# Attention block with GroupNorm: the inverse of the softmax sums computed on 128 x 4 elements instead of 128 x 512

## The chip, the cores and the metric

The kernel runs on one core of one Trainium2 chip. The metric is the device time of one execution in microseconds (us); lower is better. Beside the timed runs there is one execution taken by the hardware profiler, and all rows below are from it. Engines: PE is TensorE's matmul, PEld its weight load, DVE is VectorE, ACT is ScalarE, POOL is GpSimd and SP is SyncE, which only sends transfers here.

## The reference

Sixteen images of 512 channels by 32 x 32 positions (1024 tokens) pass through one attention block:

```python
h = group_norm(hidden_states, norm_gamma, norm_beta)      # 32 groups, eps 1e-6
q, k, v = conv1x1(h, wq, bq), conv1x1(h, wk, bk), conv1x1(h, wv, bv)
attn = jnp.einsum('bci,bcj->bij', qf, kf) * 512 ** -0.5
attn = jax.nn.softmax(attn, axis=2)
out = jnp.einsum('bcj,bij->bci', vf, attn)
return hidden_states + conv1x1(out, wo, bo)
```

Everything is float32. The softmax needs, for each query token i, the sum over j of the exponentials; the change is about the inverse of these 1024 sums.

## The kernel before

Before the loop the kernel folds the weights: wk with wq into one matrix, wo with wv into another, and keeps the split forms of both in DRAM (`kept_t`, `kept_v`). Each fp32 matrix is split into a high and a low part of type fp32r, and each product is three matmuls of 128x512 (L315, L316, L317: high x high, high x low, low x high). The products with T and the scores are done by a seven-product (Strassen-like) scheme, which is why there are many additions in between.

One image passes through these stages on PE, all in one stream:

- `make_t` (L375): 14 products, r = 0 and r = 1 with seven each, in the order p = 4, 5, 2, 7, 6, 1, 3; 84 matmuls. It reads `h_hi`, `h_lo` (made by ACT and DVE; `high_h`, `low_h` L747) and `w_split`. It starts p = 1 only when DVE has done the addition D3 of that r (L835).
- `make_scores` (L409): 28 products, 168 matmuls, written transposed: partitions are keys j, columns are queries i. DVE adds the products up in `scores`.
- `make_v` (L447): 96 matmuls, and `outputs_0` and `outputs_1` (L466, L483): 96 matmuls each. Half 0 is queries 0 to 511, half 1 the rest. Output n (0 to 7) is half n // 4 and channel block n % 4, and is summed in PSUM bank n.

The softmax per half: POOL takes the maximum over partitions (L290), DVE subtracts it (L927), ACT takes exponentials, and splits them (`high_p`, `low_p` L931). `add_up` (L941) adds the eight key blocks of a half on DVE into `red[:, half, :]`. POOL then adds this over the partitions with `partition_all_reduce` into `wide[:, half, :]` (L301), so that each of the 128 partitions holds the same 512 sums. `inverse` (L952) takes the reciprocal of all 128 x 512 in place. `output` (L956) multiplies each output bank by it into `scaled(n)`, a slot of `scores`; ACT adds the bias (`bias_output`, L603), and POOL sends it with an adding transfer to `out` (L307), signalling `out_stored[n]`. `out` has been filled by SP with a copy of x before (L226), which POOL waits for.

The order on each engine is written out by hand:

- DVE at the end of an image b: `add_up(b, 0)`, the four sums for the next image's h, the low parts `low_p` of half 1, `low_h(b + 1, 0)`, the last `low_p`, `add_up(b, 1)`, `inverse(b, 0)`, outputs 0 to 3, `low_h(b + 1, 1..6)`, `inverse(b, 1)`, outputs 4 to 7. Then `make_t` of the next image, where the D3 of r = 1 waits for `out_stored[4..7]`, since it writes a slot that output 5 was stored from.
- ACT at the start of an image: copy `snap("a")` of the first T product, the bias of outputs 4 and 5 of the image before, `snap("b")`, the bias of outputs 6 and 7.
- SP per image: the copy x to `out` (L226, 2 MB from DRAM to DRAM), pieces 0 and 1 of the next x after `h_split` reaches 7 (L232), pieces 2 to 5 after all eight outputs are scaled (L237; 256 KB each, the last two into `wide`), `kept_v` (L243), pieces 6 and 7, the next x in full (L252), and after the V products `kept_t` (L255, 3584 KB).
- POOL per image: two maxima, the deviation of the next image, two sums (L301), eight stores.

```python
            def inverse(b, half):
                dve.wait_ge(sum_all, count(b, 2, half + 1))
                nc.vector.reciprocal(wide[:, half, :], wide[:, half, :]).then_inc(inv_set, 1)
```

Of the kernel before, what the change touches and what calls it, by code (L numbers as in the profile page):

```python
# [13 lines left out]
P = 128  # L14
# [39 lines left out]
def attention_program(nc, x, gamma, beta, wq, bq, wk, wv, bv, wo, bo, out):  # L54
# [17 lines left out]
    TW, VW = 7 * 2 * QUARTER, 3 * 2 * C  # L72
    kept_t = nc.dram_tensor("kept_t", [P, 2, TW], F32).ap()
    kept_v = nc.dram_tensor("kept_v", [P, 2, VW], F32).ap()

    with ExitStack() as ctx:
        def sb(name, shape, dt=F32):
            return ctx.enter_context(nc.sbuf_tensor(name, [P, *shape], dt))

        def sem(name):  # L80
            return ctx.enter_context(nc.semaphore(name))
# [21 lines left out]
        chan_g, square_g, diff = sb("chan_g", [BLOCK]), sb("square_g", [BLOCK]), sb("diff", [KC])  # L103
        chan_kv, chan_g_kv = (a[:, 0:2 * KC].rearrange("p (k s) -> p k s", s=2) for a in (chan, chan_g))
        var_g, rstd, minus_half, primer = sb("var_g", [KC]), sb("rstd", [KC]), sb("minus_half", [KC]), sb("primer", [2])
        h_scale, h_shift, mean_scaled = sb("h_scale", [KC]), sb("h_shift", [KC]), sb("mean_scaled", [KC])


# [42 lines left out]
        def o_bank(n):  # L151
# [35 lines left out]
        max_step, centred, sum_step, inv_set = (sem(n) for n in ("max_step", "centred", "sum_step", "inv_set"))  # L187
        zeros_set, bn_set, chan_set, group_step, var_set, scale_step = (
            sem(n) for n in ("zeros_set", "bn_set", "chan_set", "group_step", "var_set", "scale_step"))
        o_scaled, o_done = sem("o_scaled"), sem("o_done")  # L190

        block = ctx.enter_context(nc.Block())
# [6 lines left out]
        def count(b, per_image, step):  # L199
            return b * per_image + step  # L200
# [3 lines left out]
        @block.sync  # L204
        def _(sp):
            for o in range(KC):
                sp.dma_start(wo_raw[:, o, :], w_d["o"][:, o, :]).then_inc(wo_in[o], 16)
            for o in range(KC):
                sp.dma_start(wv_raw[:, o, :], w_d["v"][:, o, :]).then_inc(wv_in[o], 16)
            for o in range(KC):  # L210
                sp.dma_start(wk_raw[:, o, :], w_d["k"][:, o, :]).then_inc(wk_in[o], 16)
                sp.dma_start(wq_raw[:, o, :], w_d["q"][:, o, :]).then_inc(wq_in[o], 16)
            for k in range(KC):
                sp.dma_start(full[:, k, :], x_d[0][:, k, :]).then_inc(x0_in[k], 16)

            sp.wait_ge(wvs_split, 3)
            sp.dma_start(kept_v[:, 0, :], big_hi[:, NJ:NJ + 6, :].rearrange("p a n -> p (a n)").bitcast(F32)).then_inc(kept_v_out, 16)
            sp.dma_start(kept_v[:, 1, :], big_lo[:, NJ:NJ + 6, :].rearrange("p a n -> p (a n)").bitcast(F32)).then_inc(kept_v_out, 16)
            sp.wait_ge(wt_split, 7)
            sp.dma_start(kept_t, w_split[:].bitcast(F32)).then_inc(kept_t_out, 16)  # L220
            sp.wait_ge(kept_v_out, 32)
            sp.wait_ge(kept_t_out, 16)

            def image(b, more):

                sp.dma_start(out_d[b], x_d[b].rearrange("p k n -> k p n")).then_inc(rest_in, 16)  # L226

                def piece(n):
                    k, half = divmod(n, 2)
                    sp.dma_start(pieces[n % 6],  # L230
                                 x_d[b + 1][:, k, half * HALF:(half + 1) * HALF]).then_inc(piece_in[n % 6], 16)

                if more:

                    sp.wait_ge(h_split, count(b, 7, 7))
                    for n in range(2):
                        piece(n)  # L237

                    sp.wait_ge(o_scaled, count(b, 8, 8))
                    for n in range(2, 6):  # L240
                        piece(n)
                sp.wait_ge(t_summed, count(b, 14, 14))
                sp.dma_start(w_split[:, :, 0:VW].bitcast(F32), kept_v).then_inc(wvs_in, 16)  # L243
                if more:
                    for n in range(6, PIECES):
                        sp.wait_ge(bn_set, count(b, PIECES, PIECES + n - 5))
                        piece(n)

                    sp.wait_ge(bn_set, count(b, PIECES, 2 * PIECES))
                    sp.wait_ge(s_added, count(b, 12, 12))  # L250
                    for s in range(2):
                        sp.dma_start(full[:, 2 * s:2 * s + 2, :],  # L252
                                     x_d[b + 1][:, 2 * s:2 * s + 2, :]).then_inc(full_in[s], 16)
                    sp.wait_ge(v_summed, count(b, 8, 8))
                    sp.dma_start(w_split[:].bitcast(F32), kept_t).then_inc(wt_in, 16)  # L255


            images(sp, image)
            for n in range(2 * KC):
                sp.wait_ge(out_stored[n], 16 * B)  # L260
# [421 lines left out]
        def _(dve):  # L682
# [267 lines left out]
                nc.vector.tensor_tensor(red[:, half, :], e[:, 0, :], e[:, 1, :], ALU.add).then_inc(sum_step, 1)  # L950

            def inverse(b, half):  # L952
                dve.wait_ge(sum_all, count(b, 2, half + 1))
                nc.vector.reciprocal(wide[:, half, :], wide[:, half, :]).then_inc(inv_set, 1)  # L954

            def output(b, n):  # L956
                half, c = divmod(n, KC)
                dve.wait_ge(o_summed, count(b, 8, n + 1))
                dve.wait_ge(inv_set, count(b, 2, half + 1))
                nc.vector.tensor_tensor(scaled(n), o_bank(n)[:], wide[:, half, :], ALU.mult).then_inc(o_scaled, 1)  # L960

            def image(b, more, first=False):
                make_t(b, first)
                step = 0
                for pair in range(2):
                    q0, q1 = 2 * pair, 2 * pair + 1
                    if more and pair == 0:
                        for n in range(6):
                            next_piece(b, n)
                    if more and pair == 1:  # L970
                        dve.wait_ge(bn_set, count(b + 1, PIECES, PIECES))
                    add_s(b, "C22", q0)
                    add_s(b, "C22", q1)
                    if more and pair == 0:
                        for n in range(6, 8):
                            next_piece(b, n)
                    if more and pair == 1:
                        channel_stats(b + 1)
                        group_variance(b + 1)
                    add_s(b, "C11", q0)  # L980
                    add_s(b, "C11", q1)

                    dve.wait_ge(c12_copied, count(b, 4, 2 * pair + 2))
                    dve.wait_ge(s_added, count(b, 12, ADD_AT["C11", q1]))
                    for j in (q0, q1) if pair else (q1,):
                        maximum(b, step, j)
                        step += 1
                    add_s(b, "C21", q0)
                    add_s(b, "C21", q1)
                    dve.wait_ge(s_added, count(b, 12, ADD_AT["C21", q1]))  # L990
                    for j in (KC + q0, KC + q1):
                        maximum(b, step, j)
                        step += 1
                low_v(b, 0)
                low_v(b, 1)
                centre(b, 0, 0)
                centre(b, 0, 1)
                low_v(b, 2)
                centre(b, 0, 2)
                low_v(b, 3)  # L1000
                centre(b, 0, 3)
                for g in range(4):
                    low_p(b, 0, 2 * g)
                    low_p(b, 0, 2 * g + 1)
                    low_v(b, 4 + g)
                    if more and g == 2:
                        affine(b + 1)
                for g in range(4):
                    centre(b, 1, g)
                add_up(b, 0)  # L1010
                if more:

                    dve.wait_ge(sum_step, count(b, SUM_STEPS, 3))
                    for n in range(4):
                        sum_h(b + 1, n)
                for j in range(NJ - 1):
                    low_p(b, 1, j)
                if more:
                    low_h(b + 1, 0)
                low_p(b, 1, NJ - 1)  # L1020
                add_up(b, 1)
                inverse(b, 0)

                dve.wait_ge(sum_step, count(b, SUM_STEPS, SUM_STEPS))
                for n in range(KC):
                    output(b, n)
                if more:
                    for n in range(1, 7):
                        low_h(b + 1, n)

                    dve.wait_ge(h_split, count(b + 1, 7, 7))
                inverse(b, 1)
                for n in range(KC, 2 * KC):
                    output(b, n)

# [28 lines left out]
```

## Time and profile before

| | us |
|---|---|
| median of 3 runs | 2062.42 |
| the runs | 2062.42, 2062.47, 2057.86 |
| the profiled execution's own time | 2057.07 |
| its span | 2055.4 |

Busy shares of the span: PE 98%, PEld 81%, DVE 79%, ACT 46%, POOL 16%. The granted clock is full after the first slices of the span. The PE time of an image is about 122.4 us, so 16 images make up nearly the whole span. A matmul row in the trace lasts 0.39 us while the next starts 0.227 us after it, because matmuls are pipelined; gaps are therefore seen in the start times, and in the length of a stage, not in the busy share.

### The profile page before, as it was taken

How to read it: one execution, taken by the hardware profiler on the slowest of the kernel's cores; microseconds unless marked ns; L12 is line 12 of the kernel's file. 1: busy time of each engine (PE TensorE's matmuls, PEld its weight loads, DVE VectorE, ACT ScalarE, POOL GpSimd, SP SyncE). 2: the span in 40 equal slices, each digit the busy share in tenths (PEclk: the TensorE clock that was granted, in tenths of full speed). 3: DMA queues.
4: the chain of work that ended last, by engine and by line, in shares of the span. 5: the costliest groups of instructions: out<-in, count | busy, mean ns of one | idle time of the engine just before them, and what ended most of it. 6: DMA issues, size and time to landing. Idle time of an engine off the chain costs nothing.

```text
span 2055.4 us, 26986 instructions
## 1 busy us (share of the span) xinstructions
PE 2014.2 (98%) x8848; PEld 1661.7 (81%) x8848; DVE 1619.7 (79%) x2112; ACT 955.4 (46%) x1427; POOL 325.2 (16%) x236
## 2 busy tenths in 40 slices
PE   7699999999999999999999999999999999999998
PEld 6488888888888888888888888888888888888886
DVE  3769697787978879697787978879697787968866
ACT  2635463452635445463453635445364443645442
POOL 1002012120201202012120202202011120201202
PEclk8799999999999999999999999999999999999999
DMA  3524335252343424335252343424335242343402
GB/s 123 222 96 143 113 153 143 85 139 108 125 135 153 101 83 146 109 153 143 86 138 112 122 133 153 106 77 150 105 153 143 98 127 112 127 128 153 93 10 41
DMA packets 57124, 248.79 MB, mean 121 GB/s; under 512 B 8208, under 2 KB 8208, under 8 KB 50192
## 3 DMA queue, kind: packets, MB, share of 16 engines
q1 hardware_dynamic: 36032, 214.97, 27.4%
q0 software_dynamic: 18432, 33.56, 10.9%
q10 hardware_dynamic: 2640, 0.01, 0.1%
q8 instruction: 10, 0.16, 0.0%
q14 instruction: 10, 0.08, 0.0%
HBM read 208.15 MB, written 73.92 MB: 137 GB/s over the span
## 4 chain that ended last, share of the span: by engine, by line
PE 91%; DMA 4%; DVE 2%; issue 1%; ACT 1%; POOL 0%; DVEq 0%; POOLq 0%; ACTq 0%
PE bank L315 30%; PE bank L317 30%; PE bank L316 30%; DMA out<-scores 4%; ACT scores L607 1%; DVE scores L835 0%; DVE h_lo L752 0%; DVE wide L954 0%; PE bank L352 0%; PE bank L350 0%; ACT room L527 0%; PE bank L346 0%; POOL out L307 0%; DVE w_split L803 0%; PE bank L326 0%
## 5 line engine op out<-in xcount | busy, mean ns | idle before, releaser
L315 PE MATMUL bank<-big_hi 128*128 128x512 f32 x1056 | 412.0, 390 | 0.8 <-DVE big_lo L760 0.8
L316 PE MATMUL bank<-big_lo,big_hi 128*128 128x512 f32 x1056 | 411.7, 390 | 0.0
L317 PE MATMUL bank<-big_hi,big_lo 128*128 128x512 f32 x1056 | 411.6, 390 | 0.0
L315 PE MATMUL bank<-big_hi,h_hi 128*128 128x512 f32 x896 | 349.8, 390 | 0.6
L317 PE MATMUL bank<-big_hi,h_lo 128*128 128x512 f32 x896 | 348.7, 389 | 0.0
L316 PE MATMUL bank<-big_lo,h_hi 128*128 128x512 f32 x896 | 348.7, 389 | 0.0
L913 DVE TENSOR_TENSOR scores<-bank,room 128x512 f32<-128x512 f32 x192 | 131.0, 689 | 194.2 <-ACT room L640 141.3
L640 ACT COPY room<-bank 128x512 f32<-128x512 f32 x192 | 112.8, 587 | 278.6 <-PE bank L317 278.6
L315 PEld LDWEIGHTS bank<-big_hi 128*128 128x128 f32 x1056 | 198.8, 188 | 42.6 <-DVE big_lo L760 1.2
L316 PEld LDWEIGHTS bank<-big_lo,big_hi 128*128 128x128 f32 x1056 | 198.8, 188 | 41.3
L317 PEld LDWEIGHTS bank<-big_hi,big_lo 128*128 128x128 f32 x1056 | 198.8, 188 | 41.2
L290 POOL PARTITION_ALL_REDUCE wide<-red x32 | 56.9, 1828 | 922.6 <-DVE red L922 922.6
L315 PEld LDWEIGHTS bank<-big_hi,h_hi 128*128 128x128 f32 x896 | 168.2, 188 | 40.1 <-issue 5.4
L315 PE MATMUL bank<-w_split,h_hi 128*128 128x512 f32 x512 | 199.2, 389 | 0.0
L316 PE MATMUL bank<-w_split,h_hi 128*128 128x512 f32 x512 | 199.2, 389 | 0.0
L317 PE MATMUL bank<-w_split,h_lo 128*128 128x512 f32 x512 | 199.2, 389 | 0.0
L315 PE MATMUL bank<-h_hi,w_split 128*128 128x512 f32 x448 | 177.5, 396 | 21.0 <-DVE w_split L803 8.3
L316 PEld LDWEIGHTS bank<-big_lo,h_hi 128*128 128x128 f32 x896 | 168.2, 188 | 34.8
L317 PEld LDWEIGHTS bank<-big_hi,h_lo 128*128 128x128 f32 x896 | 168.2, 188 | 34.8
L601 ACT CAST big_hi<-scores 128x512 fp32r<-128x512 f32 x256 | 147.8, 618 | 77.0 <-PE bank L317 75.0
L587 ACT CAST big_hi<-bank 128x512 fp32r<-128x512 f32 x128 | 75.2, 587 | 223.6 <-PE bank L317 223.5
L301 POOL PARTITION_ALL_REDUCE wide<-red x32 | 117.7, 3677 | 371.0 <-DVE red L950 357.1
(104 smaller groups left out, 3301.9 us busy)
## 6 DMA issues: line engine op xcount, KB each, us to landing
w_split<-kept_t SPq DMA_DIRECT2D x15, 3584.0 KB, 11.1
w_split<-kept_v SPq DMA_DIRECT2D x16, 3072.0 KB, 10.5
out<-scores POOLq DMA_DIRECT2D x128, 256.0 KB, 7.1
room<-in_x SPq DMA_DIRECT2D x30, 1024.0 KB, 5.9
room<-in_x SPq DMA_DIRECT2D x60, 256.0 KB, 3.6
red<-in_x SPq DMA_DIRECT2D x30, 256.0 KB, 3.4
wide<-in_x SPq DMA_DIRECT2D x30, 256.0 KB, 7.2
kept_t<-w_split SPq DMA_DIRECT2D x1, 3584.0 KB, 9.9
```

The costliest lines, as they stand in the source:

```text
L290: nc.gpsimd.partition_all_reduce(wide[:, half, :], red[:, half, :], P, MAX_ALL).then_inc(max_all, 1)
L301: nc.gpsimd.partition_all_reduce(wide[:, half, :], red[:, half, :], P, ADD_ALL).then_inc(sum_all, 1)
L315: nc.tensor.matmul(o, a_hi, b_hi, start=start, stop=False, skip_group_check=True)
L316: nc.tensor.matmul(o, a_hi, b_lo, start=False, stop=False, skip_group_check=True)
L317: return nc.tensor.matmul(o, a_lo, b_hi, start=False, stop=stop, skip_group_check=True)
L587: nc.scalar.copy(v_hi[:, j, :], bank[v_ring[j % 4]][:]).then_inc(v_high, 1)
L601: nc.scalar.copy(p_hi[:, j, :], scores[:, half * NJ + j, :]).then_inc(p_high, 1)
L607: nc.scalar.activation(scaled(n), scaled(n), ACT.Identity, bias=out_bias[:, c:c + 1]).then_inc(o_done, 1)
L640: nc.scalar.copy(snap_s(q, n), bank[alpha_s[q % 2]][:]).then_inc(s_snapped, 1)
L913: nc.vector.tensor_tensor(scores[:, o, :], bank[at][:], snap_s(q, n), ALU.add).then_inc(s_added, 1)
```

## The change

SP sends, for each half, one row of the sums (`wide[0:1, half, :]`, 512 values on partition 0) to a new tile `dealt` as 4 values on each of the 128 partitions. DVE takes the reciprocal of the 128 x 4 values. SP writes them to a row in DRAM (`inverse_d`), waits for that, and reads the row back to all 128 partitions of `wide[:, half, :]`. The outputs wait for that last transfer. SP does all this at the end of its part of the image, ahead of the next image's copy of x. `inverse(b, 0)` moves up in front of `low_h(b + 1, 0)`, and `inverse(b, 1)` in between `low_h(b + 1, 3)` and `low_h(b + 1, 4)`.

```diff
+    inverse_d = nc.dram_tensor("inverse_d", [2, HALF], F32).ap()
+        dealt = sb("dealt", [2, HALF // P])
+        sums_dealt, inv_out, inv_back = ([sem(f"{n}{half}") for half in range(2)]
+                                         for n in ("sums_dealt", "inv_out", "inv_back"))
@@ SP, image
                     sp.wait_ge(v_summed, count(b, 8, 8))
                     sp.dma_start(w_split[:].bitcast(F32), kept_t).then_inc(wt_in, 16)
+                for half in range(2):
+                    sp.wait_ge(sum_all, count(b, 2, half + 1))
+                    sp.dma_start(dealt[:, half, :], wide[0:1, half, :]).then_inc(sums_dealt[half], 16)
+                    sp.wait_ge(inv_set, count(b, 2, half + 1))
+                    sp.dma_start(inverse_d[half].rearrange("(p n) -> p n", p=P), dealt[:, half, :]).then_inc(inv_out[half], 16)
+                    sp.wait_ge(inv_out[half], count(b, 16, 16))
+                    sp.dma_start(wide[:, half, :], inverse_d[half].partition_broadcast(P)).then_inc(inv_back[half], 16)
@@ DVE
             def inverse(b, half):
-                dve.wait_ge(sum_all, count(b, 2, half + 1))
-                nc.vector.reciprocal(wide[:, half, :], wide[:, half, :]).then_inc(inv_set, 1)
+                dve.wait_ge(sums_dealt[half], count(b, 16, 16))
+                nc.vector.reciprocal(dealt[:, half, :], dealt[:, half, :]).then_inc(inv_set, 1)
             def output(b, n):
-                dve.wait_ge(inv_set, count(b, 2, half + 1))
+                dve.wait_ge(inv_back[half], count(b, 16, 16))
@@ DVE, image
                 for j in range(NJ - 1):
                     low_p(b, 1, j)
+                inverse(b, 0)
                 if more:
                     low_h(b + 1, 0)
                 low_p(b, 1, NJ - 1)
                 add_up(b, 1)
-                inverse(b, 0)
                 for n in range(KC):
                     output(b, n)
                 if more:
-                    for n in range(1, 7):
+                    for n in range(1, 4):
                         low_h(b + 1, n)
+                inverse(b, 1)
+                if more:
+                    for n in range(4, 7):
+                        low_h(b + 1, n)
                     dve.wait_ge(h_split, count(b + 1, 7, 7))
-                inverse(b, 1)
                 for n in range(KC, 2 * KC):
                     output(b, n)
```

## Rows read from the trace of the kernel before

**Rows 1.** The page, part 4: shares of the chain that ended last, by engine.

```profile
PE 91%; DMA 4%; DVE 2%; issue 1%; ACT 1%; POOL 0%; DVEq 0%; POOLq 0%; ACTq 0%
```

**Rows 2.** Stretches, PE: the T stage; length, busy (count), clock, DMA share, GB/s.

```profile
1064.14:1083.18 19.04, 19.04 (x85) 1.00 0.53 113
...
1309.77:1329.88 20.11, 19.50 (x86) 1.00 0.54 105
...
sum 293.81, PE 290.47; mean PE 19.36
```

**Rows 3.** Stretches, PE: the scores stage right after each T stage.

```profile
1944.27:1982.35 38.08, 38.08 (x170) 1.00 0.21 83
sum 572.80, PE 572.78; mean PE 38.19
```

**Rows 4.** The chain in order of time, 451 to 468 (start, us, what).

```profile
454.38 8.86 DMA out<-scores
...
463.55 0.76 DVE scores L835
```

**Rows 5.** DMA issues, 1924.23 to 1934.23: KB each, median us from issue to landing.

```profile
out<-scores POOLq DMA_DIRECT2D x4, 256.0 KB, 5.8
```

**Rows 6.** DMA issues, 1308.77 to 1318.77.

```profile
out<-scores POOLq DMA_DIRECT2D x4, 256.0 KB, 8.8
```

**Rows 7.** Groups of instructions by line: busy us, mean ns, idle before.

```profile
L954 DVE RECIPROCAL wide<-wide 128x512 f32<-128x512 f32 x32 | 107.2, 3349 | 0.5
...
L739 DVE TENSOR_TENSOR scores<-room 128x1024 f32<-128x1024 f32 x16 | 50.2, 3136 | 0.0
...
L732 DVE TENSOR_TENSOR h_shift<-vecs,mean_scaled 128x4 f32<-128x4 f32 x16 | 2.6, 162 | 0.6
```

**Rows 8.** DVE in order of time, 1015 to 1100 (start, us, operation).

```profile
1041.82 1.22 DVE L752 TENSOR_TENSOR h_lo<-room,h_hi 128x1024 fp32r<-128x1024 f32 x1
...
1048.21 3.35 DVE L954 RECIPROCAL wide<-wide 128x512 f32<-128x512 f32 x1
...
1067.15 0.75 DVE L835 SCALAR_TENSOR_TENSOR scores<-bank,t_step,scores 128x512 f32<-128x512 f32 x1 [0.20 <-PE bank L317]
...
1079.17 0.75 DVE L835 SCALAR_TENSOR_TENSOR scores<-bank,t_step,scores 128x512 f32<-128x512 f32 x1 [2.71 <-DMA out<-scores]
```

**Rows 9.** POOL in order of time, two image changes (start, us, operation).

```profile
1031.07 4.16 POOL L301 PARTITION_ALL_REDUCE wide<-red  x1 [7.57 <-DVE red L950]
1048.50 3.23 POOL L301 PARTITION_ALL_REDUCE wide<-red  x1 [13.27 <-DVE red L950]
1053.80 3.73 POOL L307 DMA_DIRECT2D out<-scores  x4 [2.07 <-ACT scores L607]
...
2037.20 3.61 POOL L307 DMA_DIRECT2D out<-scores  x4 [2.00 <-ACT scores L607]
```

**Rows 10.** SP's queue in order of time, 960 to 1100.

```profile
1020.81 0.34 SPq L255 DMA_DIRECT2D w_split<-kept_t  x1
1021.68 0.58 SPq L226 DMA_DIRECT2D out<-in_x  x1
```

**Rows 11.** DMA issues of the whole span; the third row is L230's answer.

```profile
w_split<-kept_t SPq DMA_DIRECT2D x15, 3584.0 KB, 11.1
...
wide<-in_x SPq DMA_DIRECT2D x30, 256.0 KB, 7.2
...
DMA to landing us min/median/max: 2.6/3.9/9.3
...
out<-in_x SPq DMA_DIRECT2D x16, 15.2
...
bq_s<-in_bq ACTq DMA_DIRECT2D x1, 2.0 KB, 3.7
```

**Rows 12.** DMA issues, 1051.14 to 1063.14.

```profile
room<-in_x SPq DMA_DIRECT2D x2, 256.0 KB, 3.2
```

**Rows 13.** Stretches: busy us of each engine, clock, DMA share, GB/s.

```profile
2038.00:2054.00 16.00, 9.79 (x44) 7.77 (x42) 5.59 (x5) 3.25 (x5) 6.32 (x8) 0.97 0.92 132
```

## Prediction

> **What bounds the kernel now.** I read the chain of waits first: TensorE (PE) has 91% of it and stores to `out` 4% [rows 1]. So only idle time of PE counts, and I looked for it stage by stage. In the stage of T (84 products, L367 to L398) an undisturbed image takes 19.04 us and the worst 20.11; the 15 images after the first take 293.81 us together, 8.2 us over 15 x 19.04 [rows 2]. The scores stage right after it takes 572.80 us, against 15 x 38.08 = 571.2 at the pace of the least disturbed image: 1.6 us over [rows 3]. The V and output stages, whose waits I searched in the same way, have no gap. So 9.8 us is all that any relief of PE between images can give.
>
> What causes these gaps is in the chain around one image change: a store of `out` that lands 8.86 us after its issue, then the addition of L835 (D3 of r = 1) [rows 4]; PE's next product comes at once after it. L835 writes the slot of `scores` from which a store of the second half is still reading, so it waits for `out_stored[4..7]`. The last image change, where no pieces of x follow, shows what that landing hangs on: there the four stores land in 5.8 us, in the worst image (T from 1309.77) in 8.8 us [rows 5, 6]. The DMA engines are what sets the small gaps, not VectorE. Yet VectorE is what this change relieves: two RECIPROCALs per image at 3349 ns each, 107 us in all [rows 7]. Both stand in a stretch where VectorE has one instruction after another [rows 8], but PE is busy with outputs 4 to 7 meanwhile.
>
> **The change, part by part.** Times are those of the image change at 1064.14, where the stage of T starts; other changes repeat it.
>
> *Removed.* 32 RECIPROCALs of 128x512. The replacement is 128x4; the nearest row is a 128x4 operation at 162 ns [rows 7]. VectorE saves 3.2 us twice per image. On PE this is worth 0: after outputs 4 to 7, which ended at 1066.95, the next addition waited 0.20 us for PE, to 1067.15 [rows 8]. What hides it is PE's own outputs stage (to 1064.14). Even the stores hardly move: `bias_output(4)` stands behind ScalarE's copy of the first new T product, which waits for PE.
>
> *Half 0.* Its sum is ready at 1031.07 + 4.16 = 1035.2 on POOL [rows 9]. SP has sent the load of `kept_t` at 1020.8, landed 11.1 us later [rows 10, 11], so it is free and its queue is empty: dealt at 1035.3. For a small transfer the trace has no equal. Nearest rows: a quiet 256 KB piece of x, fastest 2.6 us; a piece sent beside stores, 3.2 us; the 2 KB bias load, 3.7 us [rows 11, 12]. I take 2.6 without and 3.2 with stores in flight, the nearest in place and company; as ends 2.0 (an estimate: 2.6 less the 0.6 us of moving 256 KB) and, without stores, 3.7, with them 7.2 (the median of the pieces that land in `wide`, beside stores and behind three others [rows 11]). The row is dealt by 1037.9. The inverse stands in front of `low_h(b + 1, 0)`, at 1041.8 [rows 8], 3.9 us later, so this wait costs 0. Then out 2.6, back 2.6: 1047.3, before output 0 can start at 1048.4 (the place of the old RECIPROCAL plus 0.2). At 3.7 each VectorE idles 1 us, hidden under the same PE work.
>
> *Half 1.* The sum is ready at 1048.50 + 3.23 = 1051.7, plus 0.2 [rows 9]. Dealt +2.6: 1054.5. VectorE has by then done outputs 0 to 3 (2.5) and three `low_h` (3.4): 1054.3. Inverse to 1054.7, out +3.2 to 1058.0, back +3.2 to 1061.2. Outputs 4 to 6 follow by 1063.2; output 7 waits for PE's last product anyway, to 1065.2, still 1.8 us before the 1066.95 of before. Behind the two new waits of VectorE stand `low_h` 4 to 6 and outputs 4 to 7; PE asks for the fifth `low_h` 5.4 us into T. Cost 0. With 3.7 for each leg and the port loss below, outputs end at 1066.6, still in time. At the far end (3.7, 7.2, 7.2) the return lands at 1070.9 and L835 (r = 0) ends at 1074.2, where the product that needs it (p = 1, the sixth) is due 6.8 us into T, at 1070.9: 3.3 us of PE per image.
>
> *Port.* POOL's second sum ran beside a RECIPROCAL with one input; now it runs beside outputs 0 to 3. Beside POOL's first sum, L739 (two SBUF inputs) took 3136 ns on average [rows 7], and an operation of its shape undisturbed takes 1.22 us (the L752 of rows 8), so the loss is between 0 and +2.0 us. I take 0, since an output reads one operand from PSUM. The Trainium skill, SBUF — State Buffer, "Who interferes with whom", says that a VectorE instruction with two SBUF inputs contends with a GpSimd instruction that reads SBUF; by that rule, too, the loss is 0, and L739's row agrees with it.
>
> *SP's queue.* Here lies what decides. SP does not only gain 3 transfers per half. The copy of x to `out` (2 MB, DRAM to DRAM) for the next image stands behind them now. It used to go at 1021.68, landing 15.2 us later: 5.0 us after `kept_t`, in a stretch where nothing but `kept_t` wants the engines [rows 10, 11]. It now goes right after the return of half 1 is sent: 1058.0 + 0.4 = 1058.4, among the stores. I make a ledger in us of all 16 engines. A store: 16 x 0.92 / 8 = 1.84 [rows 13]. A 256 KB load: (11.1 - 2.6) x 256 / 3584 = 0.6 [rows 11]. The copy: 5.0. The stores of half 0 can leave POOL at 1052.0 instead of 1053.80 [rows 9], data flowing 1.6 us later. Work up to the first store of half 1, whose data flow at about 1069.6: 4 x 1.84 + 0.6 (return) + 5.0 + 6 x 0.6 (pieces) = 16.6, in 16.0 us without a hole, since the copy arrives before half 0's stores are through. So 0.6 us is left over. Before, the pieces 2 to 5 were sent only after output 7 (from 1066.95), and about 1.8 of their 2.4 us were left. The stores of half 1 land about 1.2 us earlier. Image 1064.14 is without a gap with L835 at 1079.17, 15.0 us into T; the stalled one of rows 4, whose T starts at 447.66, has it at 15.9. So 0.9 earlier clears the usual gap.
>
> *Sum.* -9.8 us (rows 2 and 3) x 1. At the very end: outputs 4 to 6 of the last image wait for the round trip. Before, the first of the eight last stores left at 2037.20 [rows 9]; with data 1.5 us later and no hole, 8 x 1.84 [rows 13] end at 2053.4. The sum of half 1 is ready at 2037.20 - 2.00 = 2035.2 [rows 9]; + 2.6 + 0.2 + 3.2 + 3.2 = 2044.4, and stores at 2046. The last four then occupy the engines from 2047.5 for 4 x 1.84, to 2054.9: about +1.4. Total -8.4.
>
> The profiled execution took 2057.07 us (span 2055.4, 1.7 around it); the three runs shown are 2062.42, 2062.47 and 2057.86, so it lies 5.4 under their median. I put the same step under the median: 2062.42 - 8.4 = **2054**.
>
> The Trainium skill, DMA: Bandwidth & Descriptors, "Anatomy of one DMA — SWDGE (gpsimd) path", gives each transfer about 2.0 us of fixed cost, most of it the receipt of the written data; by it the three legs would be 6 us instead of my 9.0, and the copy would start about 1.2 us sooner, which changes nothing in the sum. Its section "Why small descriptors are slow (HBM only)" speaks against the change, as the outward leg writes 128 runs of 16 bytes; no row here shows such a write.
>
> **The rivals.**
> 1. *Forecast, 0.45*: the gaps at L835 close; 2054 (2047 to 2056).
> 2. *No change, 0.27*: legs of about 3.7 us (as the bias load) put the copy 1.0 to 1.5 us later; the 1.2 us of the ledger is used up, gaps stay as they are. The small removal of VectorE work was never on the path. 2062.4 + 1.4 (end) = 2064, or a few us less. For it: rows 1 and 8. Against it: the legs of rows 12.
> 3. *Slower, 0.28*: the copy pushes the stores of half 1. It decides from 1.2 us of delay on: each further us is one us of PE at each of the 14 changes with pieces. Legs of 3.7 us with the port blocked for 2.0 us put the copy at 1060.6, 2.2 late; an outward leg of 7.2 at 1064.1, 5.7 late. Midway, 2.6 late, PE loses 1.4 per change: 14 x 1.4 + 1.4 (end) = 21, giving 2083; at the far end it is 14 x 4.5 = 63. For it: stores slowed from 5.8 to 8.8 us by only 1 MB of pieces [rows 5, 6]; 2 MB more now come to the same stretch. Against it: it ends before they begin, by the ledger.
> That the change does not do what it says is excluded by the diff: the RECIPROCAL is 128 times narrower.
>
> **The numbers.** What a measurement can tell from no change is 0.3%, 6 us. The forecast clears this by 2 us only, but if the two runs at 2062 are runs with longer gaps, closing them gives more; faster 0.45. Range 2047 (all gaps closed, from the lower runs) to 2080, which takes in the nearer half of rival 3 and leaves out its far end.
>
> **What would show it.** In the profile after: the stage of T at 19.04 us in each image (rows 2) and L835 of r = 1 waiting for PE, not DMA: forecast right. The same 19.6 to 20.1: rival 2. T stages over 20.5, with DMA landings of `out` above 9 us: rival 3. The three legs' landings, the copy's issue time within an image and the start of the outputs 4 to 7 test the steps. A wait of PE for `h_lo` or for `out` products, or a longer outputs stage, would prove the cover for the VectorE waits wrong.

## The result, and the profile after

The changed kernel takes 2073.28 us (median of 5 runs, 2070.86 to 2075.53) against 2062.42 us before (5 runs, 2057.86 to 2063.1). The ratio is 1.0058, 95% interval 1.0043 to 1.0074: slower by 0.6%, inside the stated range of 2047 to 2080, but in the direction opposite to the forecast of 2054: that of rival 3. The profiled execution took 2071.31 us, span 2069.6, so 14.2 us more than the profiled one of before.

The chain of waits of the changed kernel, by engine, has the same shape as [rows 1], with DMA at 5% instead of 4%:

```profile
PE 90%; DMA 5%; DVE 1%; issue 1%; ACT 1%; POOL 0%; POOLq 0%; DVEq 0%; ACTq 0%
```

The T stages of images 1 to 15 (stretches, PE; columns as in [rows 2]), the good and the bad ones of the same execution and the sum:

```profile
327.54:347.02 19.48, 19.41 (x86) 1.00 0.69 188
...
1068.77:1088.47 19.70, 19.50 (x85) 1.00 0.68 186
...
1562.91:1583.54 20.63, 19.52 (x86) 1.00 0.69 191
...
1810.25:1831.35 21.10, 19.50 (x86) 1.00 0.70 199
1934.84:1953.88 19.04, 19.04 (x86) 1.00 0.57 132
sum 301.27, PE 291.94; mean PE 19.46
```

The sum is 301.27 us where [rows 2] has 293.81: +7.5. The scores stages take 573.0 against 572.8 [rows 3], the V and output stages exactly what they took. From the start of the last T stage to the end of the span it is 2069.6 - 1934.84 = 134.8 us, before 2055.4 - 1925.23 = 130.2: +4.6. The rest, 2.0 us, lies before the end of the T stage of the first image, which comes at 98.5 us before and at 100.4 after. Over the profiles of all twelve kernels here it comes at 98.5 to 103.9, in no order that an edit explains, so these 2 us are not counted to the change; with one profile of each kernel that is not shown.

So two places lose. SP's queue in order of time, at the image change whose T stage starts at 1068.77, shows why (the number is the issue time):

```profile
1039.89 0.49 SPq L265 DMA_DIRECT2D dealt<-wide  x1
1046.65 0.35 SPq L267 DMA_DIRECT2D inverse_d<-dealt  x1
1048.08 0.32 SPq L269 DMA_DIRECT2D wide<-inverse_d  x1
1056.39 0.48 SPq L265 DMA_DIRECT2D dealt<-wide  x1
1058.96 0.33 SPq L267 DMA_DIRECT2D inverse_d<-dealt  x1
1064.98 0.32 SPq L269 DMA_DIRECT2D wide<-inverse_d  x1
1065.90 0.64 SPq L231 DMA_DIRECT2D out<-in_x  x1
```

Read it as gaps. Half 0 needs 1.4 us from its outward leg (L267) to the return leg (L269), and so it does in all 16 images. Half 1 needs 6.0 here, and 5.1 to 7.3 over the 16 images. Between 1056.24 and 1059.99 POOL sends the four stores of half 0, so half 1's outward leg runs beside them. The DMA issues of that kernel from 1055.77 to 1067.77 have the landings:

```profile
out<-scores POOLq DMA_DIRECT2D x4, 256.0 KB, 6.6
room<-in_x SPq DMA_DIRECT2D x2, 256.0 KB, 9.0
wide<-inverse_d SPq DMA_DIRECT2D x1, 256.0 KB, 3.4
dealt<-wide SPq DMA_DIRECT2D x1, 2.0 KB, 2.2
inverse_d<-dealt SPq DMA_DIRECT2D x1, 2.0 KB, 6.0
out<-in_x SPq DMA_DIRECT2D x1, 9.0
```

The first leg takes 2.2 us, the return 3.4, the outward one 6.0 (7.0 at the change at 1810.25). Everything behind it is late: the copy of x (L231) leaves 2.9 us ahead of T, and VectorE waits for the return.

What the late copy does to the stores of half 1 stands in the packets that the trace lists. In both kernels POOL sends these stores 3.4 to 6.7 us into T. At the 14 changes with pieces their first data packet goes 5.4 to 6.3 us into T before, and 6.8 to 8.8 after; the last packet of the copy, which had landed long before T in the kernel before, now ends 4.8 to 6.7 us into T. The last packet of the stores ends at 14.1 to 15.6 before and at 14.9 to 16.6 after, and D3 of r = 1 starts at 14.8 to 16.2 before and 15.6 to 17.2 after. The time from issue to landing hardly shows it: the median of the four is 7.3 to 8.8 us before and 7.9 to 9.2 after. VectorE in order of time, same change:

```profile
1058.76 0.17 DVE L968 RECIPROCAL dealt<-dealt 128x4 f32<-128x4 f32 x1
...
1068.51 2.48 DVE L974 TENSOR_TENSOR scores<-bank,wide 128x512 f32<-128x512 f32 x4 [6.20 <-DMA wide<-inverse_d]
...
1084.59 0.75 DVE L849 SCALAR_TENSOR_TENSOR scores<-bank,t_step,scores 128x512 f32<-128x512 f32 x1 [3.49 <-DMA out<-scores]
```

The RECIPROCAL of 3.35 us is now 0.17 us, and 6.2 us of waiting stand in its place. Outputs 4 to 7 end at 1070.99, 2.2 us into T (1.9 to 3.6 over these 14 changes); before it was 2.8. The last row is [rows 8]' L835 (now L849): it still waits for the stores.

### The profile page after: what moved, and what is told of

Its sections match the earlier page's. It is cut to its first block, busy times and chain, and to the rows that moved or that the text cites. A ratio compares the mean times of both kernels' runs of the same rounds, so it can differ in the third digit from the quotient of the medians.

```text
span 2069.6 us, 27112 instructions
## 1 busy us (share of the span) xinstructions
PE 2016.7 (97%) x8848; PEld 1662.1 (80%) x8848; DVE 1515.5 (73%) x2112; ACT 955.6 (46%) x1427; POOL 323.5 (16%) x236
## 4 chain that ended last, share of the span: by engine, by line
PE 90%; DMA 5%; DVE 1%; issue 1%; ACT 1%; POOL 0%; POOLq 0%; DVEq 0%; ACTq 0%
PE bank L329 30%; PE bank L331 30%; PE bank L330 30%; DMA out<-scores 5%; ACT scores L621 1%; DVE scores L849 0%; DVE h_lo L766 0%; PE bank L366 0%; PE bank L364 0%; ACT room L541 0%; PE bank L360 0%; POOL out L321 0%; DVE w_split L817 0%; PE bank L340 0%; DVE big_lo L806 0%
## 5 line engine op out<-in xcount | busy, mean ns | idle before, releaser
L304 POOL PARTITION_ALL_REDUCE wide<-red x32 | 56.9, 1828 | 931.8 <-DVE red L936 931.8
L588 ACT COPY scores<-bank 128x512 f32<-128x512 f32 x96 | 56.4, 588 | 265.1 <-PE bank L331 260.4
## 6 DMA issues: line engine op xcount, KB each, us to landing
w_split<-kept_v SPq DMA_DIRECT2D x16, 3072.0 KB, 10.5
```

The source lines that it names most:

```text
L304: nc.gpsimd.partition_all_reduce(wide[:, half, :], red[:, half, :], P, MAX_ALL).then_inc(max_all, 1)
L588: nc.scalar.copy(scores[:, snap_t[name], :], bank[alpha_t[r]][:]).then_inc(t_snapped, 1)
```

## The experiments

Theory A: the outward leg of half 1 is slow because it runs beside half 0's stores; through SP's order it makes the copy of x late, and the copy then holds up the stores of half 1, on which the D3 of r = 1 and PE wait; at the end of the last image the same leg holds the outputs. Rival B: what costs is VectorE's wait for the return. Each ratio is taken against runs of the kernel before that belong to the same group of kernels, so its median differs a little from group to group.

**e1_copy_late.** The kernel before with the copy moved:

```diff
-                sp.dma_start(out_d[b], x_d[b]...).then_inc(rest_in, 16)
+                sp.wait_ge(h_split, count(b, 7, 7))
+                sp.dma_start(out_d[b], x_d[b]...).then_inc(rest_in, 16)
                 if more:
-                    sp.wait_ge(h_split, count(b, 7, 7))
```

> The kernel before, with one thing changed: the copy of x to out (2 MB) is sent when h_split is complete, 3 us before the T stage, about where the changed kernel sends it. RECIPROCALs, order of VectorE and everything else as before. Theory A (the copy, sent among the stores, is what costs): landing of half 1's stores rises, the T stages of images 1 to 15 sum to 300 to 304 us (before 293.8, changed kernel 301.3), time 6 to 10 us over before. Rival B (the late return of the inverse to VectorE costs): nothing moves, within 3 us of before.

Measured: 2066.27 us against 2059.58, ratio 1.0031 (1.0020 to 1.0043), that is 6.4 us. The copy left 2.9 us ahead of every T stage (3.1 in the last image). The T stages of the profiled execution sum to 297.14 us, 3 us short of what was expected:

```profile
1189.50:1209.10 19.60, 19.54 (x85) 1.00 0.70 187
1312.59:1333.13 20.54, 19.53 (x86) 1.00 0.70 191
...
sum 297.14, PE 292.13; mean PE 19.48
```

The landing of half 1's stores did not rise as expected (8.1 to 8.7 us), but their first data packet went 6.8 to 8.6 us into T, as in the changed kernel. The late copy alone, with no other part of the change, costs about half of the loss: 0.31% of 0.58% by the timed runs, 3.3 of 7.5 us by the T stages of the profiled execution, which was the fastest of its seven. It left at one fixed place; in the changed kernel it leaves up to 1.3 us later.

**e2_copy_first.** The changed kernel with the copy put back in time:

```diff
                     sp.dma_start(w_split[:].bitcast(F32), kept_t).then_inc(wt_in, 16)
+                    sp.dma_start(out_d[b + 1], x_d[b + 1]...).then_inc(rest_in, 16)
```

(the first image's copy goes ahead of the loop, the one at the start of each image is gone)

> The changed kernel, with the copy of x to out put back to where it was in time, right after kept_t and ahead of the six transfers of the sums. Theory A: T stages back to 293 us or less, the end of the last image still 4 us later than before (the outward leg beside stores stays at 6 us), time -2 to +4 us against before. Rival B: T stages stay near 301 us and the time 10 us over before.

Measured: 2060.59 us against 2059.58, ratio 1.0010 (1.0001 to 1.0019). T stages:

```profile
1067.35:1086.38 19.03, 19.03 (x85) 1.00 0.52 114
...
1558.76:1579.27 20.51, 19.50 (x86) 1.00 0.57 119
...
sum 293.20, PE 290.05; mean PE 19.34
```

That is [rows 2]' level, while outputs 4 to 7 are as late as in the changed kernel. So the late return is not what lengthens the T stages over before; it can only be what keeps the gain of an early end away. The end stretch, from the start of the last T stage to the end of the span, is still 134.3 us (2064.4 - 1930.10).

**e3_recip4.** The kernel before, with a narrow RECIPROCAL and no transfers; 508 of each 512 columns are left uninverted:

```diff
-                nc.vector.reciprocal(wide[:, half, :], wide[:, half, :]).then_inc(inv_set, 1)
+                nc.vector.reciprocal(wide[:, half, 0:4], wide[:, half, 0:4]).then_inc(inv_set, 1)
```

> The kernel before, with each RECIPROCAL over 4 of the 512 columns only: the other columns of the sums stay uninverted, so the outputs are scaled wrongly; no transfer is added. It measures what 3.2 us less VectorE work twice per image is worth by itself. By the prediction's steps: outputs 4 to 7 end when PE has done the last product, pieces 2 to 5 leave about 2 us earlier, and the T stages fall below 293.8 us by up to 8 us; the end is unchanged. If VectorE's work never was on the path and the pieces' start does not matter either, 0 +- 2 us.

Measured: 2049.54 us, ratio 0.9955 (0.9942 to 0.9969). Every T stage is without a gap:

```profile
1796.08:1815.12 19.04, 19.04 (x86) 1.00 0.52 110
1918.48:1937.52 19.04, 19.04 (x86) 1.00 0.41 56
sum 285.60, PE 285.60; mean PE 19.04
```

VectorE's time is worth 10 us though no wait of PE ever named a RECIPROCAL. Outputs 4 to 7 end 0.9 us into T instead of 2.8, so pieces 2 to 5 are through sooner, and half 1's stores land in 5.4 to 6.7 us at the changes with pieces, against 7.3 to 8.8 before.

**e4_pieces_late.** The kernel before, pieces 2 to 5 moved behind the wait for the T stage:

```diff
-                    sp.wait_ge(o_scaled, count(b, 8, 8))
-                    for n in range(2, 6):
-                        piece(n)
                 sp.wait_ge(t_summed, count(b, 14, 14))
+                if more:
+                    for n in range(2, 6):
+                        piece(n)
```

> The kernel before, with pieces 2 to 5 of the next x sent after the T stage instead of beside the stores of half 1. If the 1 MB of pieces is what keeps the landing of these stores past its due time, they land in about 5.8 us as at the last image change, every T stage takes 19.04 to 19.1 us, and the time is 8 to 10 us under before. If the stores are slow by themselves, no change.

Measured: 2050.9 us, ratio 0.9955 (0.9941 to 0.9968); the T stages sum to 285.61 us. So the gaps of the kernel before are the meeting of 1 MB of pieces with four stores, as [rows 5, 6] had suggested. This kernel, one moved loop, beats both the kernel before and the changed one.

**e5_stores_held.** The changed kernel, the stores of half 0 behind the outward leg of half 1:

```diff
+                pool.wait_ge(inv_out[1], count(b, 16, 16))
                 pool.wait_ge(rest_in, count(b, 16, 16))
```

> The changed kernel, with POOL holding the four stores of half 0 until the outward leg of half 1 has landed. Theory A (the outward leg is slow because those stores run beside it: 6 us against 1.4 quiet): it lands in 1.4 to 2.2 us, SP sends the copy about 4.5 us sooner in the image, outputs 4 to 7 end with PE's last product; at the end the last store leaves 1 us after before's instead of 10 us, so the stretch from the last T stage to the end is 130 to 131.5 us instead of 134.8. T stages: the stores start 3 us later but the copy goes earlier, 293 to 299 us. Time 0 to +5 us against before. Rival (the leg is slow by itself, through its 16-byte runs): the leg still takes 5 to 6 us and everything gets later still, +15 us or more.

Measured: 2153.53 us, ratio 1.0463 (1.0449 to 1.0477). The first half of the expectation held: the outward leg lands in 1.4 us in 15 images and in 2.9 in the last, so it is slow beside the stores, and its rival is out. The second half, 0 to +5 us, missed by 90, and the end stretch took 134.2 us instead of 130 to 131.5. The DMA in the 7.5 us before T (1099.5 to 1107), where copy and stores are both under way, tells why:

```profile
DMA packets 192, 2.39 MB, mean 319 GB/s; under 512 B 16, under 2 KB 16, under 8 KB 160
## 3 DMA queue, kind: packets, MB, share of 16 engines
q1 hardware_dynamic: 176, 2.36, 99.8%
q0 software_dynamic: 16, 0.03, 2.3%
```

Queue q1 is SP's, q0 is POOL's stores. SP's transfers (the return leg of half 1, then the copy) take 99.8%, and the stores, issued at 1099.33 to 1103.1, move 0.03 MB. The two do not share the engines evenly. Of the 192 packets 160 are under 8 KB; the other 32 are the whole copy of 2 MB, 64 KB each, and the trace lists 2.4 to 4.0 us for one of them, against 0.18 us for a store's packet of 2 KB. Sixteen of the large packets start from 1101.60 to 1103.38. Then 16 packets of the stores go, and 0.16 us after the start of each of these one of the other sixteen large packets starts. So the queues take turns, but a turn of the copy moves 32 times what a turn of a store moves. The Trainium skill, DMA: Bandwidth & Descriptors, "Queues, rings and completion order", says that an engine takes turns between queues packet by packet. The packets listed here agree: one packet of a store between two of the copy.

The stores land after 13.8 us, and then D3 of r = 0, which waits for half 0's stores and had never been late enough to matter, is the new wait, 10.5 us into T where PE wants it at 6.8. The loss is more than that wait. The T stage of this change (length, busy, granted clock, DMA share, GB/s):

```profile
1107.02:1133.40 26.38, 22.03 (x86) 0.87 0.62 138
```

Over the whole execution PE waited 64.3 us for D3. The busy time of the T stages is 321.3 us against 291.9 in the changed kernel: these 29 us go to the clock, which is granted at 0.50 for 3 to 7 us in each of the 14 changes with pieces (see e10 for what that does to a matmul).

**e6_copy_first_held.** Both edits of e2 and e5.

> The two changes together: the copy of x to out sent right after kept_t, and the stores of half 0 held until the outward leg of half 1 has landed. Theory A: both of the losses are gone and what is left is the early end of outputs 4 to 7, which the run with the narrow RECIPROCAL showed to be worth 10 us: T stages 285.6 to 287 us, end stretch 130 to 131.5, time 6 to 10 us under before. Rival: T stages near 293 as with the copy alone moved, time as before.

Measured: 2051.64 us, ratio 0.9964 (0.9950 to 0.9977). The T stages sum to 285.60 us; the end stretch is 132.3 us (2049.8 - 1917.54), 0.8 over what was expected. The same held stores that cost 95 us beside the copy cost the T stages nothing without it; they may be what the end stretch has over the 129.4 to 129.6 of e8 and e9.

**e7_two_hops.** e2 with the outward leg split:

```diff
-                    sp.dma_start(inverse_d[half].rearrange("(p n) -> p n", p=P), dealt[:, half, :])...
+                    sp.dma_start(red[0:1, half, :], dealt[:, half, :]).then_inc(in_row[half], 16)
+                    sp.wait_ge(in_row[half], count(b, 16, 16))
+                    sp.dma_start(inverse_d[half:half + 1], red[0:1, half, :])...
```

> The changed kernel with the copy sent first, and the outward leg in two hops: the 128 runs of 16 bytes go to one row in SBUF (red, partition 0), and that row goes to DRAM in one contiguous transfer. If the write to DRAM beside the adding stores is what is slow, half 1's first hop lands in 2 to 3 us and its second in 5 or more; if it is the many short runs, the first takes 5 us or more and the second 1.5 to 3. Either way the return is 2 to 5 us later than in the copy-first run and the time 2 to 40 us over before, since outputs 4 to 7 pass their due time.

Measured: 2060.52 us, ratio 1.0013 (1.0003 to 1.0022). DMA issues in the 15 us before T at 1062.36:

```profile
dealt<-wide SPq DMA_DIRECT2D x1, 2.0 KB, 2.5
red<-dealt SPq DMA_DIRECT2D x1, 2.0 KB, 5.1
```

The hop of 128 runs of 16 bytes takes 5.1 us although its target is SBUF (4.9 to 6.2 over the images), so a write to DRAM is not needed for it to be slow. The contiguous 2 KB to DRAM behind it took 1.15 us from its issue to SP's next one, where 1.5 to 3 was expected. It met only the last 0.8 us of the stores' packets, so it does not show what such a transfer costs in their midst. The Trainium skill, DMA: Bandwidth & Descriptors, puts the cost of small descriptors down to HBM ("Why small descriptors are slow (HBM only)"); here the row into SBUF is nearly as slow as the one into DRAM.

Where the time goes can be read from the packets that the trace of the changed kernel lists. On quiet queues the 128 packets of 16 bytes run from 0.8 to 1.0 us after the issue, and SP goes on at 1.4. In images 0 to 14, beside the stores, the first one runs 1.5 to 2.7 us after the issue, the last at 2.9 to 5.9, and SP goes on at 5.1 to 7.3. While they run, one packet of a store starts right behind one of 16 bytes, and the next of 16 bytes comes 0.16 us later: 8 such turns are 1.3 us (an estimate, with 128 packets spread over 16 engines). This accounts for a part. Why the first packet comes late, and why 1.3 us pass at the change at 1068.77 between the last packet and SP's next issue where it is 0.4 on quiet queues, is not settled.

**e8_last_plain.** e2, and in the last image half 1 is inverted in place (its outputs wait for `inv_set`, which the diff below leaves out):

```diff
-                for half in range(2):
+                for half in range(2 if more else 1):
                     sp.wait_ge(sum_all, count(b, 2, half + 1))
...
+                if more:
                     inverse(b, 1)
+                else:
+                    dve.wait_ge(sum_all, count(b, 2, 2))
+                    nc.vector.reciprocal(wide[:, 1, :], wide[:, 1, :]).then_inc(inv_set, 1)
```

> The changed kernel with the copy sent first, and the second half of the last image inverted in place over all 128 x 512, without the transfers. By theory A the 4 us that the end of the last image lost (134.3 against 130.2 us from the last T stage) are the wait of outputs 4 to 7 for the outward leg: they come back, 129.5 to 130.5, and the T stages stay at 293 +- 2. Time 2 to 5 us under the copy-first run, -3 to +1 against before.

Measured: 2055.4 us, ratio 0.9983 (0.9974 to 0.9993), 5 us under e2. The end stretch is 129.4 us. The T stages came out at 289.8 us, 1 us below the expected band; the start differs too, so only the end is read from this run. What the end looked like in the changed kernel, SP's queue:

```profile
2044.84 0.48 SPq L265 DMA_DIRECT2D dealt<-wide  x1
2047.84 0.32 SPq L267 DMA_DIRECT2D inverse_d<-dealt  x1
2054.28 0.32 SPq L269 DMA_DIRECT2D wide<-inverse_d  x1
```

and POOL's stores:

```profile
2044.69 3.63 POOL L321 DMA_DIRECT2D out<-scores  x4
2059.14 3.53 POOL L321 DMA_DIRECT2D out<-scores  x4 [10.82 <-ACT scores L621]
```

The outward leg takes 6.4 us beside the first four stores. The return then lands at PE's last product (2057.4), and all four last stores leave at once behind it; before, three of them had left at 2042.77.

**e9_half0_only.** The changed kernel with the transfers for half 0 alone (the outputs of half 1 wait for `inv_set`, left out below):

```diff
-                for half in range(2):
+                for half in range(1):
                     sp.wait_ge(sum_all, count(b, 2, half + 1))
...
             def inverse(b, half):
+                if half:
+                    dve.wait_ge(sum_all, count(b, 2, 2))
+                    nc.vector.reciprocal(wide[:, 1, :], wide[:, 1, :]).then_inc(inv_set, 1)
+                    return
```

> The changed kernel with the transfers for half 0 only; half 1 is inverted in place over 128 x 512 as before, at the changed kernel's place between low_h 3 and 4. Half 0's three legs run in a quiet stretch (1.4 to 2.2 us each) and the copy of x is sent right behind them, 20 us ahead of the T stage. VectorE keeps 3.2 us of the saving per image and outputs 4 to 6 end before PE's last product. If the losses are the outward leg beside stores (half 1) and what stands behind it, then T stages take 285.6 us as with the narrow RECIPROCAL, the end stretch 129.4 to 130.2, and the time is 8 to 11 us under before. Rival (the transfers cost by themselves, or both halves' VectorE time is needed): T stages 290 us or more, time within 4 us of before.

Measured: 2049.94 us against 2059.01, ratio 0.9953 (0.9939 to 0.9967); T stages 285.60 us, end stretch 129.6. Half the change is all gain. It keeps the new place of `inverse(b, 1)` too; in the kernel before VectorE works without a pause from `add_up(b, 1)` to output 7, so that the order alone should not end the outputs sooner, but no run has the order alone. SP's queue of this kernel before T at 1061.95:

```profile
1033.07 0.48 SPq L265 DMA_DIRECT2D dealt<-wide  x1
1039.84 0.34 SPq L267 DMA_DIRECT2D inverse_d<-dealt  x1
1041.26 0.32 SPq L269 DMA_DIRECT2D wide<-inverse_d  x1
1042.07 0.62 SPq L231 DMA_DIRECT2D out<-in_x  x1
```

The legs run in the quiet stretch, and the copy, 20 us ahead of T, meets no store.

**e10_copy_later.** The kernel before, with the copy sent later still, behind pieces 2 to 5 (its line at the start of the image is gone):

```diff
                     for n in range(2, 6):
                         piece(n)
+                sp.dma_start(out_d[b], x_d[b]...).then_inc(rest_in, 16)
                 sp.wait_ge(t_summed, count(b, 14, 14))
```

> The kernel before, with the copy of x to out sent behind pieces 2 to 5, about 5 us into the T stage, in the middle of half 1's stores (images 1 to 14; the last image's copy stays where it was). By theory A the copy is not shared with the stores but goes ahead of them for its 5 us: D3 of r = 1 comes 4 to 5 us later than before, T stages of images 1 to 14 take 23.5 to 24.5 us, time +55 to +70 us. If the engines were shared evenly, about half of that; if the copy did not matter, 0.

Measured: 2152.14 us, ratio 1.0450 (1.0433 to 1.0466): +93 us, more than the strongest expectation. T stages of images 1 to 14 take 26.1 to 28.2 us. D3 of r = 1 comes at 1134.87, 20.96 us into T, 5 to 6 us later than before: that is the expected part. The other 2 us are in the clock column (stretches, PE: length, busy, granted clock, DMA share, GB/s):

```profile
1124.00:1129.00 5.00, 5.00 (x24) 1.00 1.08 414
1129.00:1135.00 6.00, 1.40 (x7) 0.84 0.64 112
1135.00:1138.00 3.00, 2.33 (x6) 0.50 0.00 0
1138.00:1141.00 3.00, 3.00 (x11) 0.69 0.00 0
1141.00:1144.00 3.00, 3.00 (x15) 1.00 0.69 197
```

After 5.3 us without work PE is granted 0.50, the 1.2 GHz level; its matmuls start 0.43 us apart instead of 0.227 until 1139.7. Ten matmuls at 0.2 us more are the 2 us. In e5 the same follows a wait of 4.35 us: from 1118.33 to 1123.61 the matmuls start 0.43 us apart.

## Why the prediction was wrong

The place was the one that the prediction put in the middle ("Here lies what decides"): SP's queue and the copy that stands in it. The deciding step in it was mis-sized, and the rule by which it added up the DMA work was wrong.

- **The term that failed: "out +3.2".** Half 1's outward leg beside stores took 5.1 to 7.3 us (6.0 at the change shown, 6.4 at the end). It was priced by a 256 KB piece in 2 KB rows, which rows 12 showed beside stores; a leg of 2 KB in 16-byte runs is another kind of transfer. Quiet, it took 1.4, below the lower end of 2.0. The other legs were right: 2.2 (2.6 forecast) and 3.4 (3.2).
- **Hence the copy.** Forecast 5.7 us ahead of T; found 1.6 to 3.3 ahead in images 1 to 14. "It decides from 1.2 us of delay on" put the place about 2 us too early: the eight images with the copy 2.6 us or more ahead, which is 2.4 to 3.1 us of delay, take 19.5 to 19.9 us but for one of 20.5, mean 19.8 against 19.6 before; the six with it 2.5 us or less ahead take 20.3 to 21.1. Over the 14 changes that is +7.5 us where rival 3, midway, had 20.
- **The ledger's rule was wrong.** It added up work as if copy, stores and pieces shared the engines. e5 shows that the copy all but shuts the stores out while it lasts, by its packets of 64 KB. In the changed kernel half 0's stores escaped this, since they were through when the copy began; half 1's did not, and their data began 6.8 to 8.8 us into T where the ledger had 5.5.
- **"Rows 2 and 3 x 1", -9.8.** Not obtained, since outputs 4 to 7 ended at 2.2 us into T instead of the forecast 1.1, and pieces 2 to 5 stood behind the copy. The size was right: in e3, e4, e6 and e9 the T stages take 285.6 us, and the scores, V and output stages between them take 1.6 us less than before. That the forecast would have held with an outward leg of 3.2 us is not shown: no run has the copy 5.7 us ahead of T with half 0's stores in their place.
- **The end, +1.4.** Measured +4.6, by the same leg: the return came at the last product, not 3 us before. e8 gives it back.
- **A slip of reading:** the T stage is 84 matmuls in 14 products, not 84 products; nothing hangs on it.
- **Right:** the removal by itself acts through the pieces and stores, not through PE (e3 is worth 10 us by it), and the stores of half 1 are issued at the same place of T, 3.4 us in, in both kernels; half 0 is hidden (VectorE waited for none of its legs, and output 0 started 15.81 us ahead of T, forecast 15.7); the second sum on POOL took 3.23 us and outputs 0 to 3 took 2.48 as before, so the port loss of outputs 0 to 3 is 0, as the Trainium skill, SBUF — State Buffer, "Who interferes with whom", has it for instructions with fewer than two SBUF inputs; the copy as the thing moved that counts.

The balance, by ratios: 1.0058 as changed; 1.0010 with the copy back in its place; 0.9983 with the last image's end mended too; 0.9964 with the stores held off the outward leg (e2's copy, but not e8's end); 0.9953 with half 1's transfers left out. Rival 3, the right direction, had a chance of 0.28; it was set below the forecast because the leg on which it hung was priced near its lower end, on a row of another kind. That the measured time lies inside the range is no merit of the forecast's sum: the range took in the nearer half of rival 3.

## What to carry to other kernels

When transfers are put into a queue, list what stood behind them there, and where it will now run: here a bulk copy that nobody waited for slid from an empty stretch into a full one and cost more than the edit was about. Price a small scattered transfer by a scattered one in the same company or give it a wide bound, and take only the half of an idea whose transfers run in a quiet stretch. When two queues meet, look at the size of their packets and not only at their bytes. And a busy engine that is never waited for can still be worth 10 us, if its end releases transfers.

## What was not expected of the hardware

- 128 runs of 16 bytes land in 1.4 us on quiet queues and in 5.1 to 7.3 us beside four adding stores of 256 KB into DRAM, 4.9 to 6.2 into SBUF.
- A DRAM to DRAM copy of 2 MB goes in 32 packets of 64 KB, 2.4 to 4.0 us each. Stores in 2 KB packets on another queue move 0.03 MB in the 7.5 us that hold most of it.
- One stall of PE of 5.3 us (e10) costs 2 us more by the clock: granted 0.50 for about 4 us after it; one of 4.35 us (e5) does the same for 5.3 us. Stalls up to 1.5 us, as in the changed kernel, left the granted clock at 1.00.
